# Weight tiles laid out turned by the host: the raw tile added by VectorE, rounded by ScalarE, subtracted by GpSimd

## The reference, cut to what matters

```python
xn = layernorm(x)
s  = attention(xn)          # 32 heads of 16, 8 groups of keys and values, causal, Wq, Wkv, Wo, bias
def matmul_lora(x, w, a, b):
    return x @ w.T + (x @ a.T) @ b.T        # rank 16
gate, up = matmul_lora(xn, gate_w, ...), matmul_lora(xn, up_w, ...)      # 512 -> 1376
y = matmul_lora(silu(gate) * up, down_w, ...)                            # 1376 -> 512
out = x + s * silu(y)
```

## Time and profile before

| | |
|---|---|
| time, median of 3 runs | 1012.03 us (1011.39 to 1013.53) |
| the profiled execution's own time | 1009.25 us |
| its span | 1007.5 us, mean granted TensorE clock 0.976 |
| TensorE busy | 925.6 us, 92% |
| VectorE busy | 584.2 us, 58% |
| ScalarE busy | 486.1 us, 48% |
| GpSimd busy | 304.1 us, 30% |
| chain that ended last | TensorE 79%, VectorE 8%, ScalarE 4%, DMA 4% |

### The profile page before, as it was taken

How to read it: one execution, slowest core, us unless ns; L and a number is a source line. 1 busy time by engine, 2 the same in 40 slices (tenths; PEclk the granted TensorE clock), 3 DMA queues, 4 the chain that set the end, 5 groups by cost and what they waited for, 6 DMA issues and landing times.

```text
span 1007.5 us, 18056 instructions
## 1 busy us (share of the span) xinstructions
PE 925.6 (92%) x6599; PEld 595.6 (59%) x6599; DVE 584.2 (58%) x1669; ACT 486.1 (48%) x975; POOL 304.1 (30%) x307
## 2 busy tenths in 40 slices
PE   4738699999999999999999999998999999989985
PEld 3625466666666666666666666554555555555664
DVE  6536656666666566665656575767655656640025
ACT  3402355656565556565656555656443443444211
POOL 3000023434343434343434343441111223120126
PEclk9967889999999999999999999999999999999999
DMA  6441724242424242424242433357745645335554
GB/s 230 150 110 44 248 86 136 76 143 79 141 81 133 84 129 86 122 87 122 90 117 96 120 100 116 91 143 218 204 116 157 178 143 141 91 94 155 156 158 151
DMA packets 142566, 129.01 MB, mean 128 GB/s; under 512 B 36104, under 2 KB 104296, under 8 KB 142256
## 3 DMA queue, kind: packets, MB, share of 16 engines
q1 hardware_dynamic: 142480, 127.87, 42.5%
HBM read 74.07 MB, written 53.22 MB: 126 GB/s over the span
## 4 chain that ended last, share of the span: by engine, by line
PE 79%; DVE 8%; DMA 4%; ACT 4%; issue 2%; SPq 2%; POOL 0%; POOLq 0%; DVEq 0%; ACTq 0%
PE bank L872 24%; PE o L1002 12%; PE bank L240 9%; PE s L966 9%; PE st L985 8%; PE bank L241 6%; PE bank L242 6%; DVE junk L1409 2%; PE bank L834 2%; DMA q<-scratch_q 2%; DVE neg_pad L1425 1%; PE bank L847 1%; PE bank L851 1%; DVE hid L1299 1%; DMA inv_sums<-scratch_r 1%
## 5 line engine op out<-in xcount | busy, mean ns | idle before, releaser
L1191 ACT ACTIVATE prob<-st 128x512 f32<-128x512 f32 (+1 forms) x640 | 324.3, 554 | 289.9 <-PE st L985 289.5
L1409 DVE CUSTOM_DVE_ANT_0 junk<-s,mask 128x128 bf16<-128x128 f32 (+3 forms) x512 | 229.4, 487 | 126.6 <-PE s L966 125.7
L1412 DVE TENSOR_REDUCE part_max<-s 128x1 f32<-128x512 f32 x256 | 163.7, 681 | 106.6 <-PE s L966 106.6
L484 POOL TENSOR_SCALAR_AFFINE_SELECT prob<-prob 128x512 f32<-128x512 f32 x128 | 84.2, 670 | 351.6 <-ACT prob L1191 351.1
L966 PE MATMUL s<-k,q 64*128 64x512 f32 (+3 forms) x768 | 150.3, 380 | 22.7 <-DMA q<-scratch_q 12.3
L872 PE MATMUL bank<-x_hi,w_hi 64*128 64x512 f32 (+1 forms) x704 | 151.0, 416 | 2.4 <-DVE hid L1299 1.1
L1002 PE MATMUL o<-prob,v 128*32 128x512 f32 (+3 forms) x1536 | 144.6, 494 | 0.0
L872 PE MATMUL bank<-x_lo,w_hi 64*128 64x512 f32 (+1 forms) x704 | 142.7, 392 | 0.0
L872 PE MATMUL bank<-x_hi,w_lo 64*128 64x512 f32 (+1 forms) x704 | 141.8, 390 | 0.0
L985 PE MATMUL st<-q,k 64*128 64x512 f32 (+3 forms) x768 | 136.6, 374 | 3.6 <-ACT prob L1191 3.6
L966 PEld LDWEIGHTS s<-k,q 64*128 64x128 f32 x768 | 77.4, 187 | 66.5 <-DVE part_max L1409 26.6
(11 more groups left out here) (103 smaller groups left out, 1004.1 us busy)
## 6 DMA issues: line engine op xcount, KB each, us to landing
hid_in<-scratch_hid SPq DMA_DIRECT2D x16, 1408.0 KB, 7.3
q<-scratch_q SPq DMA_DIRECT2D x64, 200.0 KB
scratch_hid<-tanh_hid_hi SPq DMA_DIRECT2D x40, 256.0 KB, 2.1
scratch_hid<-hid_lo SPq DMA_DIRECT2D x40, 256.0 KB, 2.4
scratch_q<-proj_hi SPq DMA_DIRECT2D x32, 256.0 KB
scratch_o<-o_sb SPq DMA_DIRECT2D x32, 256.0 KB
k<-scratch_k SPq DMA_DIRECT2D x32, 192.0 KB
scratch_q<-proj_lo SPq DMA_DIRECT2D x16, 256.0 KB
```

What stands on the lines that cost most here:

```text
L484: ins = pool.affine_select(out=blk, in_=blk, compare_op=ALU.is_ge, fill=0.0, base=0, pattern=[[0, REP], [1, P]], channel_multiplier=-1)
L1191: nc.scalar.activation(prob[:, job % 3, h, 0:JOB_COLS[j]], st[at % ST_BANKS][:, 0:JOB_COLS[j]], ACT.Exp, scale=float(HD) ** -0.5).then_inc ...
L1409: ins = dve.tensor_tensor_reduce(junk[:, n % S_BANKS, 0:wd], bank_[:, 0:wd], mask[:, C - wd:C], 1.0, LOWEST, ALU.add, ALU.max, part[:, h, ...
L1412: ins = dve.tensor_reduce(part[:, h, qt, dst:dst + 1], bank_[:, 0:wd], AX.X, ALU.max)
```

## The change

The host hands over the gate and up weights turned and cut in tiles (partitions carry the input dimension, 128 hidden columns per block, 2 KB in one piece for each partition), and the down weight turned, so that a raw tile in the ring has the layout of the PSUM bank. The transposes on TensorE go away. Of the fold there remain the low-rank matmuls, and the rest becomes three operations on three engines in a row: VectorE adds bank and raw tile, and writes the sum over the raw tile in the ring (`add_weight`, `add_down`); ScalarE rounds the sum; GpSimd, which had no part in this, subtracts (`low_weight`, `low_down`). The bank is free after VectorE's addition. The load that refills a ring place now waits for GpSimd's subtraction. The number of steps of each piece is unchanged.

```diff
@@ the readers that free a bank
-                        fold=(w_lo, 2 * a + b + 1), down_fold=(d_lo, a + 1), down=(y_done, a + 1),
+                        fold=(w_sum, 2 * a + b + 1), down_fold=(d_sum, a + 1), down=(y_done, a + 1),
@@ GpSimd
+            def low_weight(h, i):
+                n = 2 * h + i
+                pool.wait_ge(w_hi, n + 1)
+                pool.tensor_tensor(wl[:, h % 2, i, :, 0:rows[h]], raw_tile(n), wh[:, h % 2, i, :, 0:rows[h]],
+                                   ALU.subtract).then_inc(w_lo, 1)
+
+            def low_down(h):
+                hp = rows[h]
+                pool.wait_ge(d_hi, h + 1)
+                if h == NH - 1:
+                    pool.wait_ge(d_lo, h)
+                pool.tensor_tensor(dl[0:hp, h], ring[0:hp, (RAW_DOWN + h) % 8], dh[0:hp, h], ALU.subtract).then_inc(d_lo, 1)
@@ SyncE, load_raw
                 if before >= RAW_DOWN:
-                    wait_filled(sp, ("down_fold", before - RAW_DOWN, 0))
+                    sp.wait_ge(d_lo, before - RAW_DOWN + 1)
...
                 elif before >= 0:
-                    wait_filled(sp, ("fold", *divmod(before, 2)))
+                    sp.wait_ge(w_lo, before + 1)
@@ TensorE, fold
-                pe.wait_ge(raw_landed[n % 8], DMA * (n // 8 + 1))
                 pe.wait_ge(low_lo, 2)
                 out_ = take_bank(("fold", h, i))
                 for kt in range(KT):
-                    pe.matmul(out_[:, kt * P:kt * P + hp], ring[0:hp, n % 8, kt * P:(kt + 1) * P], ident[0:hp, 0:hp],
-                              is_transpose=True, start=kt == 0, stop=False, skip_group_check=True)
-                yield 1
-                for kt in range(KT):
                     mm = pe.matmul(out_[:, kt * P:kt * P + hp], a_gu[:, i, kt * P:(kt + 1) * P],
-                                   bT[:, i, h * P:h * P + hp], start=False, stop=kt == KT - 1, skip_group_check=True)
-                mm.then_inc(filled, 1)
-                yield 1
+                                   bT[:, i, h * P:h * P + hp], start=True, stop=True)
+                    if kt == KT - 1:
+                        mm.then_inc(filled, 1)
+                    if kt % 2:
+                        yield 1
@@ ScalarE, split_weight (split_down in the same way with d_sum)
-                wait_filled(act, key)
-                nc.scalar.activation(wh[:, h % 2, i, :, 0:hp],
-                                     bank_of(key)[:, :].rearrange("p (k h) -> p k h", k=KT)[:, :, 0:hp],
-                                     ACT.Copy).then_inc(w_hi, 1)
+                act.wait_ge(w_sum, n + 1)
+                nc.scalar.activation(wh[:, h % 2, i, :, 0:rows[h]], raw_tile(n), ACT.Copy).then_inc(w_hi, 1)
@@ VectorE, in the place of low_weight (add_down in the same way in the place of low_down)
+            def add_weight(h, i):
+                key, n = ("fold", h, i), 2 * h + i
+                dve.wait_ge(raw_landed[n % 8], DMA * (n // 8 + 1))
+                wait_filled(dve, key)
+                dve.tensor_tensor(raw_tile(n), folded(key), raw_tile(n), ALU.add).then_inc(w_sum, 1)
```

More of the change, by code:

```diff
@@ L370, in layer @@
         low_lo = sem("low_lo_done")
+        w_sum = sem("w_sum")
+        d_sum = sem("d_sum")
         w_hi = sem("w_hi_done")
@@ L430, in wait_filled, with raw_tile, folded @@
             engine.wait_ge(filled, NUMBER[key] + 1)
+        def raw_tile(n):
+            return ring[:, n % 8].rearrange("p (k h) -> p k h", k=KT)[:, :, 0:rows[n // 2]]
+        def folded(key):
+            return bank_of(key)[:, :].rearrange("p (k h) -> p k h", k=KT)[:, :, 0:rows[key[1]]]
         def projection(c, blk):
@@ L509, in background @@
                 done = 0
+                yield NUMBER_STEPS["fold", 0, 1] - done
+                done = NUMBER_STEPS["fold", 0, 1]
+                for i in range(2):
+                    low_weight(0, i)
                 for h in range(NH):
@@ L519, in background @@
                         finish(h, c)
-                yield 2 * STEPS["down_fold"]
-                low_hidden(NH - 1, NCH - 1)
-                yield (NH - 2) * STEPS["down_fold"]
+                        if c == 1 and h + 1 < NH:
+                            yield 2 * STEPS["fold"]
+                            done += 2 * STEPS["fold"]
+                            for i in range(2):
+                                low_weight(h + 1, i)
+                for h in range(NH):
+                    yield STEPS["down_fold"]
+                    low_down(h)
+                    if h == 1:
+                        low_hidden(NH - 1, NCH - 1)
                 def add(t):
@@ L591, in load_raw @@
                     h = n - RAW_DOWN
[L592 to L593 removed]
+                    dst, src = ring[0:rows[h], n % 8], down_w[h * P:h * P + rows[h]]
                 sp.dma_start(dst, src).then_inc(raw_landed[n % 8], DMA)
@@ L879, in fold_down @@
             def fold_down(h):
-                n = RAW_DOWN + h
                 hp = rows[h]
-                pe.wait_ge(raw_landed[n % 8], DMA * (n // 8 + 1))
                 pe.wait_ge(low_lo, 6)
                 out_ = take_bank(("down_fold", h, 0))
-                for kt in range(KT):
-                    pe.matmul(out_[0:hp, kt * P:(kt + 1) * P],
-                              ring[:, n % 8].rearrange("p (k h) -> p k h", k=KT)[:, kt, 0:hp], ident[:, :],
-                              is_transpose=True, start=kt == 0, stop=False, skip_group_check=True)
-                yield 1
-                pe.matmul(out_[0:hp, :], a_d[:, h * P:h * P + hp], bT_d[:, :], start=False, stop=True,
-                          skip_group_check=True).then_inc(filled, 1)
-                yield 1
+                pe.matmul(out_[0:hp, :], a_d[:, h * P:h * P + hp], bT_d[:, :], start=True, stop=True).then_inc(filled, 1)
+                yield STEPS["down_fold"]
             def down(t):
@@ L1068, in split_weight @@
             def split_weight(h, i):
-                key = ("fold", h, i)
-                hp = rows[h]
-                wait_filled(act, key)
-                nc.scalar.activation(wh[:, h % 2, i, :, 0:hp],
-                                     bank_of(key)[:, :].rearrange("p (k h) -> p k h", k=KT)[:, :, 0:hp],
-                                     ACT.Copy).then_inc(w_hi, 1)
+                n = 2 * h + i
+                act.wait_ge(w_sum, n + 1)
+                nc.scalar.activation(wh[:, h % 2, i, :, 0:rows[h]], raw_tile(n), ACT.Copy).then_inc(w_hi, 1)
             def read_gate(h, c):
@@ L1088, in split_down @@
             def split_down(h):
-                key = ("down_fold", h, 0)
-                wait_filled(act, key)
-                nc.scalar.activation(dh[0:rows[h], h], bank_of(key)[0:rows[h], :], ACT.Copy).then_inc(d_hi, 1)
+                hp = rows[h]
+                act.wait_ge(d_sum, h + 1)
+                nc.scalar.activation(dh[0:hp, h], ring[0:hp, (RAW_DOWN + h) % 8], ACT.Copy).then_inc(d_hi, 1)
             def split_wo(kb):
@@ L1299, in read_up, with add_down @@
                 dve.tensor_tensor(hid[0:hp, n % 2], bank[1][0:hp, :], gs[0:hp], ALU.mult).then_inc(up_read, 1)
-            def low_down(h):
-                key = ("down_fold", h, 0)
-                hp = rows[h]
-                dve.wait_ge(d_hi, h + 1)
-                dve.tensor_tensor(dl[0:hp, h], bank_of(key)[0:hp, :], dh[0:hp, h], ALU.subtract).then_inc(d_lo, 1)
+            def add_down(h):
+                key, hp, n = ("down_fold", h, 0), rows[h], RAW_DOWN + h
+                dve.wait_ge(raw_landed[n % 8], DMA * (n // 8 + 1))
+                wait_filled(dve, key)
+                dve.tensor_tensor(ring[0:hp, n % 8], bank_of(key)[0:hp, :], ring[0:hp, n % 8], ALU.add).then_inc(d_sum, 1)
             def low_wo(kb):
@@ L1471 @@
     arrays["in_L0_attn_Wo"] = np.ascontiguousarray(arrays["in_L0_attn_Wo"].reshape(heads).transpose(2, 0, 1, 3).reshape(D, D))
+    for name in ("gate_w", "up_w"):
+        wide = np.zeros((D, NH * P), np.float32)
+        wide[:, 0:F] = arrays[f"in_L0_ffn_{name}"].T
+        arrays[f"in_L0_ffn_{name}"] = np.ascontiguousarray(wide.reshape(KT, P, NH, P).transpose(2, 1, 0, 3))
+    arrays["in_L0_ffn_down_w"] = np.ascontiguousarray(arrays["in_L0_ffn_down_w"].T)
     arrays["in_low_a"] = beside(ffn["gate_a"], ffn["up_a"])
```

18 lines of the change are left out of this document (4 added, 14 removed).

## The result

The changed kernel takes **1056.82 us** (median of 5 runs, 1054.76 to 1057.68) against 1012.03 us for the one before (5 runs, 1011.1 to 1013.53): ratio 1.0436, 95% interval 1.0421 to 1.0452. It is slower, as forecast, but by 44.8 us and not by 17.6; the time lies outside the range. The profiled execution took 1057.06 us with a span of 1055.2 us, 47.7 more than before.

A forecast was written before the change was run, and what follows sets the result against it. TensorE's queue was taken as the bound. Hidden tiles +12.1, down folds +5.5 and first tile 0 made +17.6 us: 1026.9 against the profiled execution, 1029.6 us against the median, range 1014 to 1038.

The forecast's parts named there:

- the chain first addition, rounding, exponentials, score pair: Fold of tiles 1 to 10: rounding waits for VectorE's addition, so exponentials and TensorE's next score pair start 1.23 us late.
- the walk: The prediction's op-by-op timing of the folds, using earlier-trace durations, each op at the later of its queue and operand.
- GpSimd's work in the hidden tiles at nothing: Hidden tiles: GpSimd's added subtractions, 1.289 us each, fit into its idle time and cost nothing.
- 0.115 us a transpose: TensorE's queue: each removed transpose takes 0.115 us; 132 of them are 15.2 us if TensorE never waited.
- the last wait of the down folds for L518: End of the down folds: the first down product waits for GpSimd's subtraction, at 708.9 instead of 703.44.
- nine tiles of 1.23 and the last of 1.0: +12.1 us: Folds of tiles 1 to 10: each delays TensorE's score pair, never made up later, with the transposes' saving included.
- Theory 2: Posed after the result, not in the prediction: idle time and absence of the transposes' work together make TensorE's clock fall.
- the clock held 1.00 at 24.2 of 28: Down folds before the change: clock stayed full with TensorE busy 24.2 of 28 us; cited against the SyncE and clock rival.
- The down folds: Loop of addition, rounding, exponentials and score pair runs later, first down product delayed: +5.5 us, bounds +2.0 and +11.3.
- SyncE becomes the bound in the down folds, and TensorE's clock falls: Down folds: late loads or half clock add 5 to 10 us, 1035 to 1040 us; slower than forecast, chance 0.13.
- The transposes' time is simply given back: Whole kernel: removed transposes shorten TensorE's queue, at most 15.2 less 1, 998 us; chance of faster 0.08.

The follow-up runs named there:

- dve_sub: Changed kernel with the subtraction of hidden tiles 1 to 10 back on VectorE: 1056.46 us, ratio 1.0425 to the kernel before.
- no_turn: Kernel before without the hidden tiles' transposes, raw weights left out of the sum so the output is not the layer's: 1009.12 us, ratio 0.9974.
- late_half: Kernel before with only gate and up changed, ScalarE's roundings later, two identity transposes per hidden tile's half as filler: 1013.32 us, ratio 0.9997.
- late_filler: Changed kernel with later roundings in hidden tiles and down folds, plus four identity transposes ahead of the low-rank matmuls in both: 1020.64 us, ratio 1.0073.
- late_both: Changed kernel with ScalarE's hidden-tile roundings later in its queue and down roundings one pair later: 1023.63 us, ratio 1.0109 to the kernel before.
- late_hidden: Changed kernel with ScalarE's two roundings of a hidden tile moved later in its queue: 1032.03 us, ratio 1.017 to the kernel before.
- stall2: Kernel before with ScalarE's first rounding of tiles 1 to 10 done two more times: 1034.19 us, ratio 1.0211.
- filler: Changed kernel with four identity transposes, output overwritten, ahead of the low-rank matmuls in each gate and up fold: 1047.07 us, ratio 1.0326 to the kernel before.
- stall4: Kernel before with ScalarE's first rounding of tiles 1 to 10 done four more times: 1063.86 us, ratio 1.0502.
- down_only: Kernel before with the change made for the down matrix alone: 1025.81 us, ratio 1.0132.
- down_filler: Kernel before with only the down matrix changed, plus four identity transposes ahead of each down piece's low-rank matmul: 1022.71 us, ratio 1.0107.

## Why the prediction was off

**Right.** The bound (TensorE's queue), the chain first addition, rounding, exponentials, score pair, and each of its times within 0.1 us at tile 2; that no second stall follows (the second addition and rounding come 0.2 us earlier than the walk has them); GpSimd's work in the hidden tiles at nothing (`dve_sub`); 0.115 us a transpose (0.91 us of busy time for eight by `no_turn`, 0.92 predicted); the last wait of the down folds for L518; that the transposes' time is not given back. One reading is a little off: the walk starts a consumer 0.1 us after its producer, while its own rows have 0.03 to 0.05 us (204.68 to 204.71, 205.66 to 205.71), which makes its chain some 0.1 us late in all.

**The step that failed** is the first term, "nine tiles of 1.23 and the last of 1.0: +12.1 us". It priced the stall at its own length and kept everything behind it at the pace of the earlier trace rows, that is, with the clock at 1.00: the cost of the clock behind the stall is put at nothing there, without a reason. The fold-to-fold distance was to grow by 1.2 and grew by 2.99. The parts, by the runs: idle time in the period went from 0.47 to 2.24 us, +1.8 (predicted +2.1); busy time less 1.55 for one fall would be 48.3 instead of 49.07, -0.8 (predicted -0.9). The sum of these two is about +1.0, close to the 1.23. The rest, 2.0 us a fold, is the clock: 1.5 us where it falls once, 2.6 where the period shows 0.94 (3 of 9, 53.2 against 52.1 for one fall). By six of the one and three of the other it is 1.9 us on average, some 19 over ten folds; less the 0.2 us a fold by which stall and saving came out under 1.23, that is about the 17.7 us by which the hidden tiles (29.8) pass their term (12.1). (In all, the profiles' 47.7 us exceed the sum of 17.6 by 30.1: these 17.7, 5.7 in the down folds, 5.7 behind them and 1.0 ahead of the first hidden matmul.) That split adds up prices found in different runs, since the changed kernel has no period without a fall to look at. The profile of the kernel before is also of an execution 2.8 us under that kernel's median, which is why the two profiles differ by 47.7 us where the medians differ by 44.8.

**Why it fell in every period.** A stall of 1.2 us alone and the missing work alone each let the clock fall in some folds. The nine periods of each profile, with TensorE's wait before the score pair as it stands at tile 2, and its idle time in a usual period:

| ScalarE's queue | TensorE's work in the fold | idle, us | falls in |
|---|---|---|---|
| as before | transposes (before) | 0.5 | 0 |
| as before | none (`no_turn`) | 0.8 | 2 |
| roundings later | half filler (`late_half`) | 0.6 | 0 |
| roundings later | filler (`late_filler`) | 0.5 | 0 |
| roundings later | none (`late_both`, `late_hidden`) | 0.7 | 4, 6 |
| stall of 1.2 (`stall2`) | transposes | 1.7 | 4 |
| stall of 1.3 (`filler`) | filler | 1.8 | 3 |
| stall of 1.7 (changed kernel) | none | 2.2 | 9 |
| stall of 2.5 (`stall4`) | transposes | 2.9 | 9 |

Idle time alone doesn't order the rows: 0.7 us without the work brings as many falls as 1.7 us with it. So Theory 2 fits best, but it is not shown in full. Each count is of one execution; where the work goes some idle time comes in its place, so no run takes away the work alone; and a stall of 1.7 us with the transposes left in was not run, so that this stall alone would already make all nine fall is not ruled out (1.2 us gave four, 2.5 us nine). That the falls belong to the fold is plainer: in all these traces they begin 2.9 to 6.6 us behind the period's first low-rank matmul and nowhere else in the period.

The kernel before sits where a little more idle time or a little less work already tips some folds; the change does both at once. The prediction used "the clock held 1.00 at 24.2 of 28" as evidence against a fall in the down folds, and never asked the question for the hidden ones, where TensorE is 99% busy over the group and the idle time sits in one place. The Trainium skill (TensorE: Matmul & The Clock Gate, Part 1) says that the clock is set by how busy TensorE has been recently; the traces agree, with 1.00 in the nine periods before and 0.97 or 0.94 after. Why among equal folds of one run some fall and others not (`late_both`) is left open.

**The down folds**, +5.5 predicted with bounds of +2.0 and +11.3: +11.2 in the profile, +11.9 in `down_only` (40.95 us from the last hidden matmul to the first down product, 29.09 before). The walk had both ends right. The first pair comes 2.4 us later behind the stretch's start than before (4.94 against 2.53; 2.5 in the walk), and from the last pair to the down product it is 4.14 us (4.25 in the walk, 1.64 before). It failed between them: from the first of these pairs to the last, 23.25 us by the walk, 22.93 before and 29.20 measured. These two stretches, before and after:

```profile
678.87:701.80 22.93, 20.61 (x142) 10.91 (x143) 17.84 (x60) 14.51 (x31) 3.78 (x6) 1.00 0.73 213
```

```profile
712.08:741.28 29.20, 24.64 (x105) 10.09 (x107) 16.81 (x56) 14.93 (x31) 14.71 (x14) 0.58 0.64 193
```

TensorE is busy 4.0 us longer there with 37 instructions less, and idles only 2.2 us more. Over the whole stage the prediction had 19.6 us busy of 33.5, so 13.9 idle; measured are 26.88 busy of 38.28 and 11.4 idle. So the walk, which kept the durations of the earlier trace rows and with them the full clock, didn't miss idle time but the clock, here as in the hidden tiles. How much of the 6.3 us the clock makes is not isolated by a run: `down_filler` raised it from 0.63 to 0.77 and the stretch was 1.7 us shorter.

The rival "SyncE becomes the bound in the down folds, and TensorE's clock falls" was half right: the clock fell to 0.62, but SyncE was not the bound. The loads of the hidden values went out at 727.72, well ahead of the product at 745.42, which waited for GpSimd. The additive form of the rival's price, 5 to 10 us on top of the forecast, was right in size for this stage; the hidden tiles then add their 17.7 on top.

The 5.7 us behind the down folds have no term in the prediction. Part of them is in the stretch at 0.86 shown above, and part may be the fast execution that the profile of the kernel before shows (its mean clock, 0.976, is the highest that any of its runs has; behind the first down product it is 0.99, against 0.97 in the changed kernel); the end of the program varies by itself, 53 to 58 us from the last context to the last matmul among kernels that don't differ there, so the 1.8 is not put down to the change.

**"The transposes' time is simply given back"**: `no_turn` is this rival with nothing in its way, and wins 2.6 us (0.2 to 5.1), not 10. Of 0.91 us a tile, 0.4 becomes idle time, 0.5 is given back, and the two falls of the clock (1.5 us each) take part of that again.

## What to carry to other kernels

When TensorE is the bound and its clock is at 1.00, a stall costs its own length plus what the clock does behind it; here a stall of under 2 us brought 1.5 to 2.8 us more wherever the clock fell. Work taken off TensorE in a place where it already has to wait for another engine is worth little: here about half of it became idle time, and the clock fell in folds where it had held. Before moving an instruction ahead of an exponential, copy or mask that feeds TensorE, look at which queue it lands in; moving ScalarE's roundings four steps back in its queue was worth 25 us, while the engine that did the hidden tiles' subtraction made no difference.

## What was not expected of the hardware

- A fall of the granted clock has a nearly fixed price in this kernel, whatever brought it on: 1.5 us (49.0 and 50.5, 49.3 and 50.8, 50.8 and 52.2 for the same instructions without and with). Where the period's clock is 0.94 it is 2.6 to 2.8 us (53.6 against 50.8 in `stall2`).
- Useless TensorE work made a kernel faster: 88 transposes whose output is overwritten took the changed kernel from 1057 to 1047 us. In the version with later roundings they removed every fall in the hidden tiles; 44 more in its down folds raised the clock from 0.66 to 0.90 and took no time off (32.7 and 34.0 us).
- In equal code with equal idle time, the clock fell in some folds and not in others, in one execution.
